# Bias rows added by GpSimd instead of TensorE, first keys staged in a second buffer, and one group of transposes moved, in a two-layer gated attention kernel

## The reference

```python
x = x + tanh(g_xattn[0]) * causal_attention(layernorm(x), ctx, ctx)          # 16 heads of 32
x = x + tanh(g_ffn[0])   * ffn_ternary_weights(layernorm(x))                 # hidden 2048, silu gate
x = x + tanh(g_xattn[1]) * cross_attention(layernorm(x), ctx)
x = x + tanh(g_ffn[1])   * bitlinear_ffn(layernorm(x))                       # hidden 2048, 8-bit activations
# the parts of cross_attention that matter here (all 256 context rows are image rows)
q = rms_norm(x @ q_w.T + q_b) * norm_q_w
k = rms_norm(ctx @ k_img_w.T + k_img_b) * norm_k_img_w
v = ctx @ v_img_w.T + v_img_b
out = (softmax(q k^T / sqrt(32)) v) @ o_w.T + o_b
```

## Time and profile before

| | |
|---|---|
| three timed executions | 1132.94, 1133.54 (median), 1133.76 us |
| the profiled execution | 1134.22 us, its span 1132.4 us |
| mean granted TensorE clock | 0.997 of full speed |
| busy | TensorE 1091.6 us, VectorE 835.8, ScalarE 566.9, GpSimd 74.9 |

### The profile page before, as it was taken

One profiled execution on the slowest core, in us unless ns is written; L12 is line 12 of the kernel. 1 busy time (PEld: TensorE's weight loads), 2 busy tenths in 40 slices (PEclk: granted clock), 3 DMA queues, 4 the chain that ended last, 5 costly groups with the idle time before them and its releaser, 6 DMA issues.

```text
span 1132.4 us, 25473 instructions
## 1 busy us (share of the span) xinstructions
PE 1091.6 (96%) x10310; PEld 666.1 (59%) x10418; DVE 835.8 (74%) x1448; ACT 566.9 (50%) x918; POOL 74.9 (7%) x180
## 2 busy tenths in 40 slices
PE   8799999999999999999999999899999999999998
PEld 3455555555777777777777655455454545454544
DVE  5788888788777657666565667886868778777886
ACT  3676767775433323333333452455554637372754
POOL 0000000000000000000001012010101010101010
PEclk9899999999999999999999999999999999999999
DMA  9565564543112011021010201101010101000001
GB/s 365 175 197 171 185 186 148 167 128 123 66 39 56 30 38 38 20 75 26 31 57 20 84 2 38 38 2 57 1 58 1 56 2 29 10 11 10 11 10 38
DMA packets 29267, 79.24 MB, mean 70 GB/s; under 512 B 3040, under 2 KB 3296, under 8 KB 28896
## 3 DMA queue, kind: packets, MB, share of 16 engines
q1 hardware_dynamic: 29152, 77.61, 21.2%
HBM read 65.02 MB, written 12.58 MB: 69 GB/s over the span
## 4 chain that ended last, share of the span: by engine, by line
PE 89%; issue 3%; ACT 3%; DVE 2%; DMA 1%; POOL 0%; SPq 0%; ACTq 0%; DVEq 0%; POOLq 0%
PE bank L586 10%; PE bank L587 10%; PE bank L690 10%; PE bank L545 10%; PE bank L672 9%; PE bank L793 8%; PE bank L425 5%; PE bank L823 5%; PE bank L781 5%; PE bank L743 3%; PE bank L762 3%; PE bank L477 2%; PE bank L510 2%; PE bank L498 2%; PE bank L450 2%
## 5 line engine op out<-in xcount | busy, mean ns | idle before, releaser
L586 PE MATMUL bank<-ARENA,W 128*128 128x256 f16 x1024 | 227.3, 273 | 0.7 <-issue 0.7
L587 PE MATMUL bank<-ARENA,W 128*128 128x256 f16 x1024 | 227.3, 273 | 0.0
L1000 ACT ACTIVATE ARENA<-bank 128x512 f32<-128x512 f32 (+3 forms) x143 | 92.9, 687 | 82.3 <-PE bank L425 33.2
L545 PE MATMUL bank<-ARENA 128*128 128x512 f32 x256 | 119.7, 611 | 1.2 <-DMA ARENA<-in_wkv 1.2
L793 PE MATMUL bank<-W,ARENA 128*128 128x512 bf16 x493 | 115.1, 379 | 3.6 <-DVE ARENA L1661 1.7
L690 PE MATMUL bank<-ARENA 128*128 128x512 f32 x256 | 116.9, 599 | 0.0
L672 PE MATMUL bank<-W,ARENA 128*128 128x512 bf16 x472 | 114.6, 379 | 2.2 <-issue 0.2
L586 PEld LDWEIGHTS bank<-ARENA,W 128*128 128x128 bf16 x1024 | 100.2, 98 | 19.1 <-issue 1.3
L587 PEld LDWEIGHTS bank<-ARENA,W 128*128 128x128 bf16 x1024 | 100.2, 98 | 18.0
L1000 ACT ACTIVATE ARENA<-ARENA 128x512 f16<-128x512 f32 x64 | 40.4, 632 | 136.9 <-DVE ARENA L1583 129.4
L1583 DVE SCALAR_TENSOR_TENSOR ARENA<-bank,ARENA 128x512 f32<-128x512 f32 x64 | 48.0, 750 | 69.7 <-PE bank L587 66.6
(11 more groups left out here) (180 smaller groups left out, 1764.7 us busy)
## 6 DMA issues: line engine op xcount, KB each, us to landing
W<-in_w SPq DMA_DIRECT2D x48, 512.0 KB, 4.1
ARENA<-in_w SPq DMA_DIRECT2D x24, 512.0 KB, 3.7
kv_store<-ARENA SPq DMA_DIRECT2D x32, 256.0 KB, 4.1
W<-kv_store SPq DMA_DIRECT2D x15, 512.0 KB, 4.2
ARENA<-in_ctxT SPq DMA_DIRECT2D x8, 512.0 KB, 3.8
X<-in_x SPq DMA_DIRECT2D x8, 512.0 KB, 5.8
ARENA<-in_ctx SPq DMA_DIRECT2D x8, 512.0 KB, 5.1
out<-X SPq DMA_DIRECT2D x16, 256.0 KB, 2.2
```

What stands on the lines that cost most here:

```text
L545: mm = pe.matmul(bank, bufA["KT"][:, b % 2 * KD + k, t * P:(t + 1) * P], W[:, k, :], start=(k == 0), stop=(k == KD - 1 and what == 1))
L586: pe.matmul(bank[:, i * S:(i + 1) * S], W0[:, at:at + P], xt_half(b, 0)[:, k, :], start=(k == 0), stop=False)
L587: mm = pe.matmul(bank[:, i * S:(i + 1) * S], W0[:, at:at + P], xt_half(b, 1)[:, k, :], start=False, stop=(k == KD - 1))
L1000: return act.activation(to, src, ACT.Copy)
```

## The change

1. The key bias is no longer a product. The row is loaded into `keep["row"]` (f32), and GpSimd adds it to each stored key tile in SBUF (`a_add_bias`), after ScalarE's copy and before the store, which now waits for `a_kb`.
2. The output bias row, times the gate, is put into `keep["row"]` in stage B, and GpSimd adds it to x in place, two tiles per batch (`c_add_bias(f)`), behind the query roots of turn f; `c_add_out` waits for it. The query bias stays a product. `split_row` is left for the query row only.
3. The key tiles of batch 0 are staged in `bufA["tmp"]`, and the first two value tiles use `bufA["kv"]` without waiting for a store.
4. `c_turn_x(3)` stands on TensorE behind `c_scores(2, 0)`, and turn 2's bank lists are changed: xt0 behind w2 in bank 6, xt1 behind qt1 in bank 5, w3 behind qt0 in bank 7.

```diff
-        places.turn(2, ("pq0 po0 w0 xt0", "po1 w1 qt1 w3", "pq1 kt0 tq1 w2", "kt1 mt tq0 qt0 xt1"))
+        places.turn(2, ("pq0 po0 w0", "po1 w1 qt1 xt1", "pq1 kt0 tq1 w2 xt0", "kt1 mt tq0 qt0 w3"))
...
+        def staged(b, i):
+            return bufA["tmp"][:, i, :] if 4 * b + i < TB else bufA["kv"][:, i % 2, :]
...
                 n = 4 * b + i
-                sp.wait_ge(s.a_kvr, n + 1)
-                sp.dma_start(kv_store[b, i // 2, i % 2, :, :], bufA["kv"][:, n % 2, :]).then_inc((s.st_kv0, s.st_kv1)[n % 2], 16)
+                if i < TB:
+                    sp.wait_ge(s.a_kb, TB * b + i + 1)
+                else:
+                    sp.wait_ge(s.a_kvr, n + 1)
+                sp.dma_start(kv_store[b, i // 2, i % 2, :, :], staged(b, i)).then_inc((s.st_kv0, s.st_kv1)[n % 2], 16)
...
-            sp.dma_start(bufA["tmp"][:, 0, :], vec[:, 0:D]).then_inc(s.ld_kb, 16)
+            sp.dma_start(keep["row"], vec[:, 0:D]).then_inc(s.ld_kb, 16)
...
-                    mm = pe.matmul(bank, bufA["KT"][:, b % 2 * KD + k, t * P:(t + 1) * P], W[:, k, :], start=(k == 0), stop=(k == KD - 1 and what == 1))
-                if not what:
-                    pe.wait_ge(s.c_bias, 1)
-                    mm = pe.matmul(bank, keep["trip"], keep["bias"][:, 0, :], start=False, stop=True)
+                    mm = pe.matmul(bank, bufA["KT"][:, b % 2 * KD + k, t * P:(t + 1) * P], W[:, k, :], start=(k == 0), stop=(k == KD - 1))
...
-                    pe.matmul(to, src[:, k, t * P:(t + 1) * P], WQ[w][:, k, :], start=(k == 0), stop=False)
-                pe.wait_ge(s.c_bias, row + 1)
-                return pe.matmul(to, keep["trip"], keep["bias"][:, row, :], start=False, stop=True)
+                    mm = pe.matmul(to, src[:, k, t * P:(t + 1) * P], WQ[w][:, k, :], start=(k == 0), stop=(w == "o" and k == KD - 1))
+                if w == "q":
+                    pe.wait_ge(s.c_bias, 1)
+                    mm = pe.matmul(to, keep["trip"], keep["qbias"], start=False, stop=True)
+                return mm
...
             c_weigh(1, 3)
-            c_turn_x(3)
...
                 c_scores(b, 0)
+                if turn == 3:
+                    c_turn_x(3)
                 d_value_gate(d, 0)
...
             def a_projected(b, i):
                 n = 4 * b + i
-                act.wait_ge((s.st_kv0, s.st_kv1)[n % 2], 16 * (n // 2))
+                if n >= 2 * TB:
+                    act.wait_ge((s.st_kv0, s.st_kv1)[n % 2], 16 * (n // 2))
                 act.wait_ge(s.a_kv, n + 1)
-                copy(bufA["kv"][:, n % 2, :], banks[bank_of_kv(b, i)]).then_inc(s.a_kvr, 1)
+                copy(staged(b, i), banks[bank_of_kv(b, i)]).then_inc(s.a_kvr, 1)
...
             def a_divide(b):
                 v.wait_ge(s.a_otr, 3 * b + 1)
+                if b == 0:
+                    v.wait_ge(s.st_kv0, 16)
+                    v.wait_ge(s.st_kv1, 16)
...
-            v.wait_ge(s.ld_kb, 16)
-            split_row(0, bufA["tmp"][:, 0, :], bufA["tmp"][:, 1, :], keep["bias"][:, 2, :])
...
             def c_add_out(b, t):
+                v.wait_ge(s.c_xb, 2 * b + t + 1)
                 v.wait_ge(s.c_po, 2 * b + t + 1)
...
-                    v.wait_ge(s.b_w1, 3 * b)
-                    split_row(2, bufB["row"], bufB["left"], bufB["pos"][:, 0:D])
+                    v.wait_ge(s.a_kb, TB * NB)
+                    v.tensor_scalar(keep["row"], bufB["row"], keep["tgate"][:, 1:2], None, ALU.mult).then_inc(s.c_bias, 1)
...
+            def a_add_bias(b, t):
+                kv = staged(b, t)
+                pool.wait_ge(s.ld_kb, 16)
+                pool.wait_ge(s.a_kvr, 4 * b + t + 1)
+                pool.tensor_tensor(kv, kv, keep["row"], ALU.add).then_inc(s.a_kb, 1)
+
             for f in range(NB):
                 pool.wait_ge(s.a_ve, f + 1)
                 inverse_root(keep["rstd"], keep["ve"], TB).then_inc(s.a_rstd, 1)
+                a_add_bias(f, 0)
+                a_add_bias(f, 1)
...
+            def c_add_bias(f):
+                pool.wait_ge(s.c_bias, 2)
+                pool.wait_ge(s.c_xn, 2 * f + 2)
+                for t in range(TB):
+                    pool.tensor_tensor(xt_of(f, t), xt_of(f, t), keep["row"], ALU.add).then_inc(s.c_xb, 1)
...
             c_queries_root(0, 1)
+            c_add_bias(0)
             c_rstd(1)
...
                 if c == 0:
                     d_line(c)
+                if f < NB:
+                    c_add_bias(f)
                 if f + 1 < NB:
                     c_rstd(f + 1)
```

More of the change, by code:

```diff
@@ L42 @@
     a_ve a_rstd a_xn a_xt a_xtr a_sc a_scr a_mhl a_mt a_mtr a_st a_ex a_pv a_pvr a_sum a_sumr a_ot a_otr a_xo
-    a_ab a_sg a_gs a_s a_r a_abs a_kv a_kvr
+    a_kb a_ab a_sg a_gs a_s a_r a_abs a_kv a_kvr
     b_ve b_rstd b_xn b_xt b_xh b_xl b_g b_gu b_sg b_h b_sq b_acc b_fold b_ss b_me b_inv b_hh b_hl b_pr b_xy b_neg b_w1
     c_ve c_rstd c_xn c_xt c_xtr c_kss c_kinv c_kn c_kt c_ktr c_sc c_scr c_mhl c_mt c_mtr c_st c_ex
-    c_pv c_pvr c_pjq c_qss c_qinv c_qn c_qt c_qtr c_po c_xo c_const c_vb c_vo c_vor c_bias
+    c_pv c_pvr c_pjq c_qss c_qinv c_qn c_qt c_qtr c_po c_xo c_const c_vb c_vo c_vor c_bias c_xb
     d_st d_line d_hw d_xr d_tq d_q d_sv d_qt d_qtr d_g d_gu d_sg d_u d_so d_tu d_u16 d_ut d_utr d_utv d_y d_res
@@ L164, in build @@
                 ("stats", (2, 6), F32), ("ve", (2,), F32), ("rstd", (2,), F32), ("mean", (2,), F32), ("ss", (3, 8), F32),
-                ("sm", (3, 4), F32), ("selc", (4, P), BF16), ("trip", (P,), BF16), ("bias", (3, D), BF16), ("cols", (12,), F32),
+                ("sm", (3, 4), F32), ("selc", (4, P), BF16), ("trip", (P,), BF16), ("row", (D,), F32), ("qbias", (D,), BF16), ("cols", (12,), F32),
                 ("nqk", (4,), F32), ("mvd", (2, 2), F32), ("statsd", (2, 6), F32), ("rstdd", (2,), F32), ("ri", (2,), F32), ("slope", (2,), F32),
@@ L378, in load_keys_of @@
                 sp.wait_ge(s.c_kt, max(0, 2 * (f - 1)))
-                sp.wait_ge(s.c_bias, 3)
+                sp.wait_ge(s.c_bias, 2)
                 sp.dma_start(keys_of(f), kv_store[f, 0, :, :, :].rearrange("t p d -> p t d")).then_inc((s.ld_k0, s.ld_k1)[f % 2], 16)
@@ L390, in sync_program @@
                 if n == 6:
-                    sp.wait_ge(s.c_bias, 2)
+                    sp.wait_ge(s.c_bias, 1)
                     sp.dma_start(bufB["row"], vec[:, 2 * D:3 * D]).then_inc(s.ld_row, 16)
@@ L684, in tensor_program, with c_product @@
             WQ = {o: bufC["wqo"][:, n, :].rearrange("p (k d) -> p k d", k=KD) for n, o in enumerate("qo")}
-            def c_product(name, f, src, t, w, row):
+            def c_product(name, f, src, t, w):
                 to, sem, value = bank_c(name, f)
@@ L696, in c_project_q @@
                 pe.wait_ge(s.c_xtr, 2 * f + t + 1)
-                c_product(f"pq{t}", f, CT, t, "q", 1).then_inc(s.c_pjq, 1)
+                c_product(f"pq{t}", f, CT, t, "q").then_inc(s.c_pjq, 1)
             def c_project_out(b, t):
                 pe.wait_ge(s.c_pvr, 4 * b + 4)
-                c_product(f"po{t}", b, bufC["OT"], t, "o", 2).then_inc(s.c_po, 1)
+                c_product(f"po{t}", b, bufC["OT"], t, "o").then_inc(s.c_po, 1)
             def c_value_bias():
@@ L1445, in a_ternary, with split_row @@
                                     ).then_inc(*own.up())
-            def split_row(n, row, left, part):
-                hi = keep["bias"][:, n, :]
+            def split_row(row, left, part):
+                hi = keep["qbias"]
                 v.tensor_copy(hi, row).then_inc(*own.up())
@@ L1783, in bias_rows @@
                     v.wait_ge(s.ld_row, 16)
-                    split_row(1, bufB["row"], bufB["left"], keep["bias"][:, 2, :])
+                    split_row(bufB["row"], bufB["left"], bufB["pos"][:, 0:D])
                 if b == 1:
```

## The result

| kernel | median, us | runs | ratio to before, 95% interval |
|---|---|---|---|
| before | 1135.07 (1132.94 to 1137.93) | 8 | |
| changed | 1128.99 (1127.54 to 1130.13) | 8 | 0.9943 [0.9929, 0.9958] |

The change makes the kernel faster by 0.57%, or 6.5 us of 1135.07; on the 1133.54 us of the three runs shown ahead this is 1127.1 us. Forecast were 1126.4 us, and a gain of 7.1. The profiled execution took 1127.54 us, with a span of 1125.5: 6.9 us less than that of before.

The account below looks back on a forecast made before the run. TensorE, busy 96% of the span, was taken as the bound. The terms 6.8 + 1.6 + 0.5 - 1.8 gave 7.1 us gained, so 1126.4 us against the median of 1133.54; range 1123.0 to 1130.5 us.

Parts of the forecast that it names:

- 1, matmuls: Key and output products on TensorE: each loses a bias matmul of 0.22 us; 31 of 32 count, 6.8 us gained.
- 3, staging and turn 1: First stage, turn 1: ScalarE's wait for the key store goes, 2.1 us arrive, less half a possible hold; net 1.6 us.
- 4, seam: Before the third turn: one bank wait is exchanged for an earlier one, value product 0.5 us earlier; bounds 0 and 1.7.
- 2, holding, turns 3 to 7: Before the query transposes: GpSimd's two additions hold VectorE, so TensorE loses 0.36 us a turn, 1.8 us in five.
- feed-forward stage: VectorE's changed row work there was costed at nothing, since TensorE sets the pace in that stage.
- Part 2, price: GpSimd's 32 additions of 128x512 f32 were taken to last 1.0 us each; 1.12 us by the skill's reference.
- d: Length of one bias addition on GpSimd, taken as 1.0 us.
- Part 2, effect: Query transposes, turns 3 to 7: VectorE, held by GpSimd, comes late, and TensorE loses what exceeds its 0.59 us in hand.
- 2d - 1.64: TensorE's loss per turn at the query transposes, turns 3 to 7: 0.36 us for additions of 1.0 us.
- 2d - 1.05: VectorE's lateness in turns 3 to 7, from two back-to-back additions starting at 812.94 against its conversions' start at 813.99.
- Part 2, the sign of being wrong: The prediction called itself wrong if VectorE's SBUF operations appeared stretched elsewhere too, beyond its conversions or query scaling in turns 3 to 7.
- the first addition holds one, up to 1.0 us: Turn 1: batch 1's first key addition may hold one of VectorE's two-input bf16 products; half of 1.0 us was taken.

Follow-up runs that it names:

- e3: The changed kernel without its staging: the first batch's keys use the old halves and ScalarE's copies wait for their stores; 1132.17 us, ratio to before 0.9973.
- e2: The changed kernel with GpSimd's output additions moved between the two query roots instead of behind the second; 1125.86 us, ratio to before 0.9922.
- e4: The kernel before with only the key and output bias matmuls taken out, so its output lacks these biases; 1130.12 us, ratio to before 0.9954.
- e6: The changed kernel with the fourth batch's tokens turned ahead of the third turn's first scores again, in the old banks; 1128.66 us, ratio to before 0.9936.
- e5: The changed kernel with each output addition done twice in a row on GpSimd, so that bias counts twice; 1131.25 us, ratio to before 0.9949.
- e7: The changed kernel with output additions between the query roots and the second batch's first key addition held until the third scores' reduce; 1126.90 us, ratio to before 0.9917.
- e1: The changed kernel run once more without any edit; 1128.34 us, ratio to before 0.9939.
- e8: The changed kernel with constant matmuls in TensorE's idle time of turn 1 and of the last turn; 1128.81 us, ratio to before 0.9929.
- e10: The changed kernel with gate and value products moved ahead of the transposes at the seam and in the tail; 1126.82 us, ratio to before 0.9924.
- e11: The changed kernel with early output additions, products ahead of transposes at seam and tail, and 5 constant matmuls in the last turn; 1124.96 us, ratio to before 0.9901.
- e9: The changed kernel with constant matmuls at three late idle places: the seam, the last turn and the tail; 1125.03 us, ratio to before 0.9900.

## Why the prediction came out right, and where it did not

The sum was right; two of its terms were not, and others were missing. That it met the measured time so closely is in part luck: the holding that cost nothing in turns 3 to 7 (1.8 us) and the larger gain of turn 1 (1.4) are offset by half-speed stretches (3.0) that the forecast does not have.

| step | forecast, us | shown |
|---|---|---|
| 1, matmuls | 6.8 (31) | 6.4: 29 by 0.22, 13 in the first stage and 16 in the third; the three ahead of the markers can't be told apart from the next row |
| 3, staging and turn 1 | 1.6 | 3.2 with these three: 3.0 the staging (e3), 0.2 the rest |
| 4, seam | 0.5 | 0.6 (e2 against e4; 0.48 by e6) |
| 2, holding, turns 3 to 7 | -1.8 | 0 (e2, e5); at the seam -0.5 (e2), not forecast |
| two turns with a shorter wait for ScalarE | none | 0.5, only with the staging |
| feed-forward stage | 0 | -0.15 |
| half-speed stretches of the late stages | none | -3.0 in the profiled run |

Together 10.0 by the markers, less 3.0: 7.0 against 6.9 measured.

- **Part 1** holds to the digit: 3.64 against 3.63 us, and e4 with nothing else changed. In e4 the three products ahead of the second marker gave only 0.1 us, so beside the store wait three were to be taken out, not one. That the engines behind cost nothing holds as well.
- **Part 2, price.** d was 1.27 us, not 1.0. The size was off, within the range; my estimate of 1.12 from the Trainium skill's "GPSIMD Engine Reference", section 3.1, was nearer. With d = 1.27 my formula gives 0.90 a turn, 4.5 in five.
- **Part 2, effect: the step that failed.** "TensorE has 0.33 + 0.26 = 0.59 in hand, so it loses 2d - 1.64 per turn." That VectorE is held and late was right; that TensorE loses by it was not. I took the wait shown behind the transposes (0.26) as the whole cover. The row under it said 1.74 us for 14 matmuls whose like, unhindered, take 1.0: they too waited, for the second half of ScalarE's exponentials. The cover was 0.33 + 0.26 + 0.6 (e2) = 1.2 us, and VectorE's lateness 2.42 - 1.29 = 1.13. Also, 2d - 1.05 took the whole overlap for held time: it would be 1.49 where 1.13 was measured. Of the two conversions only the second is held in full (1.76 us from 807.35; the first takes 0.74).
- **Part 2, the sign of being wrong.** The prediction is wrong, it said, if VectorE's operations on SBUF appear stretched elsewhere too. They do, in the changed kernel: a normalisation at 12.6 us (1.41 us instead of 0.55), a cast at 16.7 (1.50 instead of 0.42), L1716 at the seam (0.66 instead of 0.15). The last costs 0.5 us, which the sum did not have; the first two lie ahead of turn 1, and no run shows their cost.
- **Part 3.** The wait goes and VectorE is late next, as said; "the first addition holds one, up to 1.0 us" is seen at L1451 (0.96), and costs some 0.4 us (e7), near the half that I took. The term was still the one most mis-sized, 1.6 for 3.0. It compared the fourth scores alone, where 2.1 were forecast ahead of the hold and 2.63 measured with it. The other 0.6 us of the turn come behind them; no run isolates their cause. The store wait also swallowed every gain made ahead of it: with it (before, e3, e4) the second marker stands at 48.8 to 49.0 us, whether the first is at 27.15 or at 28.97. Without it the second follows the first, and that one varies by chance (27.04 to 28.24 us), with the landing of the first weights.
- **Part 4** holds, with its wait of 2.35 us (shown at e6) where the earlier trace rows had it: 719.54 - 717.1 = 2.4.
- **Not in the prediction at all:** the granted clock in the late stages. I had read it in turn 1 only, since the trace of before has no other stretch. One execution was no basis for this: other runs of before have mean clocks down to 0.991, its profiled one 0.997. Runs of before take 1133.7 to 1134.4 us at 0.997, 1136.4 to 1137.7 at 0.994 and 1138.5 to 1139.2 at 0.991 (beside e1).

What stays open: whether the change makes such stretches more frequent. By markers it is worth 10.0 us, by the medians 6.5. Of the ten profiles with the change and without fills at all three places, nine (the result's, e1 to e3, e5 to e8, e10) have one to four of 3.4 us behind 700 us; e11 has none while TensorE works. The two of before and e4 have none. But mean clocks are 0.9943 for before (29 runs, beside e1 and e5) and 0.9938 for the changed kernel (14, those of the result and e1), too near to tell. The waits ahead of the stretches in the last turn and in the tail (1.28 us; 1.61 and 0.43) are the same in both kernels. The kernel before was not run with its idle places filled. Nor is settled why two waits of TensorE for ScalarE are 0.28 us shorter in two turns (ahead of the tokens' transposes 0.28 instead of 0.56, and none instead of 0.28 ahead of a max turn): they stand at full length in before, e3 and e4, the three without the staging, and in no other run.

## What to carry to other kernels

A wait that appears need not cost anything: before pricing it, find what the engine waited for next without it, and look for waits inside groups of matmuls that last longer than their like. To judge an edit, compare the starts of one instruction per turn in both traces; that showed 0.00 us where the waits had suggested 0.6. Look in each trace whether the cause to be removed is there at all: e7 took away a hold that its yardstick e2 did not have. Where TensorE is busy 97% of the time, idle places of 1.3 to 2.4 us can cost more by the clock behind them than by themselves (1.28 us idle, then 3.0 us lost), and a few matmuls of constants there made this kernel 3.3 us faster, but only where TensorE sets the pace.

## What the runs showed of the hardware

- The granted clock falls behind idle times of only 1.3 to 2.4 us, in one execution and not in the next (1.28 us in the last turn: 0.50 in the changed kernel's profile, 1.00 in e1's). The late stretches are 3.4 us or twice that. One costs up to 1.75 us (from the last max turn to the end 87.48 us in e1 and e2, 85.73 in e9), 1.35 at the seam in e1, 3.0 for 6.8 us at 1043, and nothing at 711 in e5, where TensorE waits for VectorE behind it.
- An f32 addition of 128x512 on GpSimd takes 1.27 us; beside VectorE's conversions or two-input products it took 1.5 to 1.76 (e8).
- GpSimd holds VectorE too: a conversion of 0.69 us took up to 1.76, a product of two bf16 tiles 1.65; a reduce of one tile and instructions that read a bank were not held. Instructions on 2 elements are held as well: 1.20 and 1.12 us instead of 0.17 (e5), where a chain of them runs beside GpSimd's additions.
